# Macaron block on one core: row maxima spread evenly over the attention chunks, their first units placed further behind the projections

## The reference, cut to what matters

```python
x = x + 0.5 * ffn(layernorm(x), ...)     # 256 -> 2048 gate and up, gelu(gate) * up, 2048 -> 256 down
x = x + attention(layernorm(x), ...)     # 16 heads of 16, causal, softmax, output projection
x = x + 0.5 * ffn(layernorm(x), ...)     # the same weights as the first
# attention
att = einsum('bhqd,bhkd->bhqk', q, k) / sqrt(16)
att = where(causal, -1e9, att); att = softmax(att)
```

## Time and profile before

| | us |
|---|---|
| median of 3 runs | 1058.31 (1054.94 to 1059.23) |
| the profiled execution | 1055.69 |
| its span, first to last instruction | 1053.6 |
| PE busy | 948.1 (90%) |
| DVE busy | 621.1 (59%) |
| ACT busy | 469.9 (45%) |
| POOL busy | 232.7 (22%) |
| mean granted TensorE clock | 0.957 of full speed |

### The profile page before, as it was taken

How to read it: one execution, slowest core, us unless ns; L and a number is a source line. 1 busy time by engine, 2 the same in 40 slices (tenths; PEclk the granted TensorE clock), 3 DMA queues, 4 the chain that set the end, 5 groups by cost and what they waited for, 6 DMA issues and landing times.

```text
span 1053.6 us, 16739 instructions
## 1 busy us (share of the span) xinstructions
PE 948.1 (90%) x6726; PEld 410.9 (39%) x6726; DVE 621.1 (59%) x1008; ACT 469.9 (45%) x634; POOL 232.7 (22%) x261
## 2 busy tenths in 40 slices
PE   2879996998999999899999998999998685999998
PEld 1435553543444535224544222434322121255544
DVE  6986244654864688545788455688757574062221
ACT  2224142133227331796330998532298382933240
POOL 3744273033200440002330000042000000034140
PEclk9889998999999999999999999999999696999999
DMA  7000032006000060000230000000000000000000
GB/s 246 1 0 2 1 69 33 2 1 100 1 2 2 1 101 1 2 2 2 63 40 7 15 2 2 1 1 1 21 2 2 1 1 2 1 1 1 21 1 20
DMA packets 21803, 20.26 MB, mean 19 GB/s; under 512 B 4064, under 2 KB 21472, under 8 KB 21728
## 3 DMA queue, kind: packets, MB, share of 16 engines
q1 hardware_dynamic: 18528, 16.06, 7.9%
q10 hardware_dynamic: 3200, 3.15, 0.9%
HBM read 12.78 MB, written 6.29 MB: 18 GB/s over the span
## 4 chain that ended last, share of the span: by engine, by line
PE 74%; DVE 9%; ACT 6%; issue 5%; DMA 3%; SPq 1%; POOL 1%; ACTq 0%; DVEq 0%; POOLq 0%
PE ps L1102 11%; PE ps L1073 11%; PE ps L1074 10%; PE ps L1075 10%; PE ps L1251 10%; PE ps L1206 7%; PE ps L1103 5%; ACT inter L716 5%; PE ps L1234 5%; DVE sg L1011 2%; DVE sg L1014 2%; DMA qreg<-qk_split 2%; DVE oT L802 1%; PE ps L1218 1%; PE ps L1177 1%
## 5 line engine op out<-in xcount | busy, mean ns | idle before, releaser
L716 ACT ACTIVATE inter<-ps 128x1024 f32<-128x1024 f32 (+3 forms) x320 | 266.4, 899 | 65.9 <-PE ps L1234 51.6
L622 POOL TENSOR_TENSOR inter<-wreg,inter 128x512 f16<-128x512 f32 x112 | 129.5, 1158 | 690.4 <-ACT inter L705 690.2
L1014 DVE TENSOR_REDUCE sg<-ps 128x2 f32<-128x1024 f32 (+3 forms) x224 | 228.9, 1043 | 63.1 <-PE ps L1206 32.8
L726 ACT ACTIVATE wreg<-ps,gelu_in 128x512 f32<-128x512 f32 x112 | 77.1, 689 | 282.4 <-PE ps L1075 282.4
L1102 PE MATMUL ps<-wd,inter 128*128 128x512 f16 x512 | 171.0, 380 | 0.0
L1011 DVE TENSOR_REDUCE sg<-ps 128x1 f32<-128x512 f32 (+3 forms) x192 | 112.0, 628 | 95.5 <-PE ps L1206 64.4
L878 DVE SCALAR_TENSOR_TENSOR wreg<-ps,kappa,wreg 128x512 f32<-128x512 f32 x128 | 95.9, 749 | 106.8 <-PE ps L1075 103.9
L1251 PE MATMUL ps<-inter,v 128*17 128x512 f32 (+3 forms) x1280 | 155.6, 560 | 1.0
L1206 PE MATMUL ps<-kreg,qreg 48*128 48x512 f16 (+3 forms) x640 | 112.6, 364 | 35.7 <-DVE sg L1011 12.6
L1103 PE MATMUL ps<-wd,inter 128*128 128x256 f16 x512 | 139.6, 273 | 0.0
L1234 PE MATMUL ps<-qreg,kreg 50*128 50x512 f16 (+3 forms) x640 | 113.1, 366 | 25.8 <-ACT inter L716 14.4
(11 more groups left out here) (136 smaller groups left out, 903.6 us busy)
## 6 DMA issues: line engine op xcount, KB each, us to landing
qk_split<-oT SPq DMA_DIRECT2D x4, 1024.0 KB, 4.5
kreg<-qk_split SPq DMA_DIRECT2D x24, 128.0 KB, 4.6
qreg<-qk_split SPq DMA_DIRECT2D x24, 128.0 KB, 7.8
xres<-in_L_attn_x ACTq DMA_DIRECT2D x4, 512.0 KB, 9.0
out_x<-xres SPq DMA_DIRECT2D x4, 512.0 KB, 2.9
kreg<-in_L_ffn_up_W_packed ACTq DMA_DIRECT2D x4, 256.0 KB, 5.8
kreg<-in_L_ffn_gate_W_packed SPq DMA_DIRECT2D x4, 256.0 KB, 7.0
kreg<-in_L_ffn_down_W_packed SPq DMA_DIRECT2D x1, 1024.0 KB, 9.6
```

What stands on the lines that cost most here:

```text
L622: pool.tensor_tensor(inter[:, 1, u, :], prod_ring[:, u % 3, :], inter[:, 0, u, :], ALU.subtract).then_inc(s_inter, 1)
L716: act.activation(p_ring[:, pair % 8, :, 0:w], ps[:, 512 * b:512 * b + 1024].rearrange("p (a q) -> p a q", a=2)[:, :, 0:w], ACT.Exp, scale= ...
L1014: dve.tensor_reduce(m_part[:, r, part, col:col + 9:8], both[:, :, 0:width], AX.X, ALU.max).then_inc(s_slot_read, 1)
```

## The change

Three things change in the planner, and no instruction is added or removed; only their order differs.

1. The time from which the units of chunk c may be placed is now the estimated end of DVE's read of the second qk item plus 20.5, and no longer that of "v" plus 11.0.
2. In attention, `pace` works out after each pair how many units per pair are needed: for each later group, the units still to be done up to it, divided by the pairs until it plus 36 for each FFN pass between. The largest of these is added to `credit`, every unit put takes 1 from it, and `late` is 0.9 while the credit is at least 1, else 0.0. The counting of what is owed to the next group goes.
3. Two costs of the planner change: a gelu from 0.65 to 0.69, and an exponential from 0.19 + 2w/1200 to 0.18 + 2w/1207 (w columns in each of its two banks).

```diff
+            FFN_UNITS = 36
...
-                if kind == "v":
-                    end["stacks", n] = dve + 11.0
+                if kind == "qk" and u:
+                    end["stacks", n] = dve + 20.5
...
-                            act = gelu_end[cc, n] = max(act, pe + LAG, inter_end.get((cc, n - 3), 0.0)) + 0.65
+                            act = gelu_end[cc, n] = max(act, pe + LAG, inter_end.get((cc, n - 3), 0.0)) + 0.69
...
-            def fill_attention(until, late):
+            def pace(now, place_now):
+
+                rest, due, room = 0, 0.0, 0
+                left = {}
+                for kind, n, _ in todo:
+                    left[n] = left.get(n, 0) + (kind == "max")
+                for n in range(now + 1, NGRP):
+                    rest += left.get(n, 0)
+                    pairs = 2 * (first_step[n] - place_now[0]) - place_now[1] - 1
+                    guests = sum(FFN_UNITS for k, (kind, c) in enumerate(MAIN)
+                                 if kind == "ffn" and MAIN.index(("attention", now // NG)) < k <
+                                 MAIN.index(("attention", n // NG)))
+                    due = max(due, rest / max(1, pairs + guests))
+                return due
+
+            def fill_attention(until, credit):
                 while todo:
                     item = todo[-1]
-                    start = start_of(item)
+                    start, late = start_of(item), 0.9 if credit >= 1 else 0.0
                     if item[0] == "negate" or start <= pe + max(0.05, late) and \
                             max(start, pe) + cost_of(item) <= until + late:
+                        credit -= item[0] == "max"
                         put(todo.pop())
                     else:
-                        return
+                        break
+                return credit
...
-                            act = bank_end[b] = bank_end[b + 1] = max(act, pe + LAG) + 0.19 + 2 * w / 1200
+                            act = bank_end[b] = bank_end[b + 1] = max(act, pe + LAG) + 0.18 + 2 * w / 1207
...
-                            owed = sum(item[1] <= n + 1 for item in todo)
-                            left = 2 * (last_step - t) - hp - 1
-                            fill_attention(bank_end[2 - b], 1.0 if owed > left else 0.0)
+                            credit = fill_attention(bank_end[2 - b], credit + pace(n, (t, hp)))
```

More of the change, by code:

```diff
@@ L370, in attention @@
                 act += 1.3
+                credit = 0.0
                 for n in range(NG * c, NG * c + NG):
```

## The result

The changed kernel takes 1006.68 us in the median of 4 runs (1005.12 to 1007.15), against 1058.77 (1054.94 to 1059.55, 4 runs): a ratio of 0.9512, 95% interval 0.9486 to 0.9538. Forecast were 1009. Run again later beside three of the experiments it had 1006.22 us and a ratio of 0.9542 (0.9512 to 0.9572). The profiled execution took 1007.13 us, 48.6 less than that of before, and its span is 1005.3. One execution of e3 (5078.59 us) and one of e6 (2317.80 us) were several times as long as all others of their kernels and stand in no ratio.

A forecast was written before the change was run, and what follows sets the result against it. Bound: PE, 90% busy, with ACT's exponentials pacing attention and units forced alone before groups 14 and 15. Terms -14.9 - 2 - 41.5 + 10.2 = -48.2 on 1055.7 gave 1007.5, put at 1009 us; range 998 to 1030 (own range 999 to 1020).

The forecast's parts named there:

- The bound: Whole kernel: PE 90% busy; ACT's exponentials pace attention; units alone before groups 14 and 15 take 12.6 and 17.4 us.
- A: ffn 1 and 2: waits for the query stacks and the half clock behind them go, -14.9 us (-10.7 to -16.5).
- the case that the prediction had as its bound: A's bound of -10.7 us: the clock in ffn 1 and 2 falls as before.
- About 7 units are displaced into attention 0: ffn 2 loses about 7 units to attention 0 and gets shorter by about 2 us (0 to 4).
- rival 4: ffn 1 and 2: units placed later meet another wait of the same size; 1024 us, chance 0.04.
- B: Attention 3: nothing left to force, 161.5 to 120 us, -41.5 (bounds -48 and -20).
- C: Attention 0 to 2: 53 units beyond the free ones at 0.26 us, less group 11's 3.6: +10.2 (+1 to +17).
- 1, the pace isn't reached: Attention: credit grows unused, units are left for group 14, half of B stays; 1025 us, chance 0.10.
- 2, every unit exposed: Attention 0 to 2: each extra unit stalls ACT by its full 1.4 us cycle; 1069 us, chance 0.04.
- 3, the clock falls in attention 0 to 2: More units between pairs bring the low clock, 104 us over 192 pairs; 1113 us, chance 0.03.
- 5, nothing changes: Whole order nearly as before, the paces being covered by what was filled anyway; 1056 us, chance 0.03.

The follow-up runs named there:

- e3: The kernel before with only the two planner costs changed (0.69 for a gelu, 0.18 + 2w/1207 for an exponential): 1061.0 us, ratio 1.0045.
- e6: The changed kernel with `late` always 0.9 in attention, so no pace at all: 1024.96 us, ratio 0.9706.
- e2: The changed kernel with the later first units and the two costs taken back, so the pace alone: 1020.76 us, ratio 0.9672.
- e1: The kernel before with only the later first units (20.5 us after the second qk item is read): 1048.16 us, ratio 0.9936.
- r2: The changed kernel with 23.0 instead of 20.5 for chunk 0 alone: 1005.58 us, ratio 0.9542.
- e9: The changed kernel, but behind the second pair of a step a unit may be late only from a credit of 2: 1001.81 us, ratio 0.9497.

## Why the prediction was right

**The bound, and where the time lay.** Right: the loss was 30.0 us of units standing alone before groups 14 and 15, the crowded units of groups 13 and 14, and the clock behind them, and all of it went. e2 has it with the pace alone. e1 and e3 show the same mechanism the other way round: one more such place between groups 10 and 11, with a single forced unit, and 10.7 and 8.6 us more for attention 2.

**A, first units later: -14.9 and -2 predicted, -15.2 measured.** The waits went as worked out (2.1 us stay where 1.6 were expected; the landing moved after all, from 166.2 to 167.1). The clock behind them didn't come back whole: in ffn 1 it is at 0.61 for 4.3 us behind the wait that stays, so of the 4.2 us some 2.5 went, near the case that the prediction had as its bound. With 3 units fewer (0.8 us) that makes 13.5; the other 1.7 us are not traced. "About 7 units are displaced into attention 0" was mis-sized: 3 are, since ffn 2 still holds 28 units of chunk 1 (31 before) beside the 8 that spill over from ffn 1. That alone the part gives only some 7 us, for another reason than rival 4's, wasn't foreseen: this term held only because both parts came together.

**B, attention 3: -41.5 predicted, -46.7 measured.** Mis-sized by the baseline. The prediction took 30.0 us from group 12 and 29.6 from group 15 as the time of an undisturbed group. The first has 3.4 us at the low clock and the second 6.4 (its window says 0.89). At full clock a group takes 28.4 us (the earlier trace rows against the 841.30 row above: the same instructions, 29.60 and 28.40).

**C, the earlier chunks: +10.2 predicted, +15.2 with what group 11 gives back, by stages 2.7 + 11.2 + 1.3.** Mis-sized in attention 1: 11.2 where 5.2 were worked out. The price was read against the same 30.0: against 28.4, group 13's ten more units cost 4.1 us (its length is 32.5), not 2.6, so 0.41 each. And the prediction multiplied a mean rate of 0.63 with one price, where the price rises: groups 5 to 7 had 33 units in 48 pairs, 0.69, and before 16 (max matmuls of these three groups below, after and before). 17 more units cost 8.5 us, 0.50 each. In groups 8 to 10, at 0.57, 15 more cost 5.0, 0.33 each. Some 1.4 us of the 11.2 is the clock, which has 6.8 us at the low level in attention 1 in this profile and 3.4 in that of before; in attention 0 it is the other way round (none, and 3.4 before), so that its units cost about 1 us more than the 2.7 says.

```profile
431.90:482.00 50.10, 11.48 (x66) 3.10 (x66) 1.00 0.01 2
442.80:484.40 41.60, 5.70 (x32) 1.55 (x32) 1.00 0.01 1
```

The errors of B and C had opposite signs, 5.2 and 5.0 us. So had the two small ones: 1.7 us missing before attention 0, and 1.8 gained in ffn 3, 4 and 5, where nothing was forecast (ffn 3 alone holds 4 units fewer). So the sum was right to 0.4 us of the profiled execution by luck as much as by working: -48.2 worked out, -48.6 measured. The mechanism needed no luck.

**Rivals.** 1, the pace isn't reached: wrong, 20, 40 and 55 units are what was worked out (21, 40, 55). 2, every unit exposed: wrong for the change, but its price of 1.1 us per unit exists between 0.58 and 0.75 units per pair (e6). 3, the clock falls in attention 0 to 2: wrong, the windows have 1.00, 0.95 and 0.98 there, and even group 9 of e6, with 18 units in 26.9 us, has 1.00. The Trainium skill's rule on cycling through PSUM banks (TensorE: Matmul & The Clock Gate, "A second HAM failure mode: psum-queue depth-cycling") isn't borne out at these rates. 4, the first part gives nothing: wrong in the changed kernel, 15.2 us before attention 0. 5, nothing changes: wrong.

What stays open: how much of the 46.7 us in attention 3 is the low clock alone. No experiment kept the bunches and the clock apart. Three profiles allow an estimate for group 14, whose units stand at the same places before, in e3 and in e1 (exponentials, in this order):

```profile
831.70:870.90 39.20, 28.92 (x32) 0.85 0.01 1
839.70:876.70 37.00, 28.83 (x32) 0.92 0.01 1
826.10:866.00 39.90, 28.94 (x32) 0.83 0.01 1
```

Between 0.85 and 0.92 lie 2.2 us, so at 1.00 it would take about 35: some 4.5 us of the clock and 6 of the units. Groups 12 and 15 were 1.4 and 1.2 us longer than at full clock. That makes about 7 us of the 46.7; what the clock did inside the two stretches of units alone isn't known.

## What to carry to other kernels

Where a planner may only put work into gaps and makes up for the rest by force, look at the places where it forces: one late item costs its whole chain (here 5 to 7 us) and often the clock behind it, and a small change of cost or place can make such a spot hundreds of microseconds away. Spread deferrable work by need, but read the price per item as a curve: here free at 0.44 units per pair, 0.3 us for each unit more at 0.57, 0.5 at 0.69 and 1.1 between 0.58 and 0.75 where the units crowd. Two groups with the same count can still differ by how closely the units follow each other. And take the time of an undisturbed stretch only from a window at full clock.

## What the runs showed of the hardware that was not expected

- The stretches at the low clock are few, and their places differ between runs of the same order. The changed kernel's lasted 3.4, 6.8 and 3.4 us between 100 and 1000 us. In r2 and e9 one stands at the start of attention 0 instead of in ffn 1, in r2 without the wait before it and in e9 with one of 1.2 us. The same kernel run again had 3.4 us where the first profile had 6.8 (attention 1 66.3 and 67.7 us). That is 1 to 2 us of a run which no edit explains.
- A stretch at the low clock can cost much less than half its length where ACT sets the pace. Group 15, which has no units, took 29.6 us before with 6.4 us of it, against 28.4 without: 1.2 us, where half would be 3.2. Group 12 with 3.4 us of it took 29.6 us (e9) against 28.1 without in the changed kernel, 1.5 us, which is nearly half.
